# Routed experts, attention, routed experts on one core: the order of work at the start of the first expert loop, and where the first plane of results is added in the last stage

## What is computed

```
x = x + 0.5 * ffn(layernorm(x))
x = x + attention(layernorm(x))      # 16 heads of 16
x = x + 0.5 * ffn(layernorm(x))      # same weights as the first

ffn(x):                              # M = 2048 tokens, H = 256, 16 experts
  t      = x * rsqrt(mean(x*x) + eps) * norm_w
  logits = t @ gate_w.T + gate_b ;  4 best of 16, softmax over the 4 -> G
  h      = t @ w1[e].T + b1[e]       # 512 wide: a = even, b = odd columns
  act    = min(a,7) * sigmoid(1.702*min(a,7)) * (clip(b,-7,7) + 1)
  y      = act @ w2[e].T + b2[e]
  return x + sum over the 4 chosen e of G[e] * y
```

## Time and profile before

| what | us |
|---|---|
| three runs | 806.88, 807.64, 803.91 (median 806.88) |
| the profiled execution, its own time | 807.14 |
| its span in the trace | 804.4 (granted TensorE clock 0.976) |
| TensorE matmuls busy | 702.1 (87%) |
| VectorE busy | 586.4 (73%) |
| ScalarE busy | 440.1 (55%) |
| GpSimd busy | 403.1 (50%) |
| chain that ended last: TensorE / time in which the engine waited for nothing shown / GpSimd / VectorE | 30% / 8% / 8% / 8% |

### The profile page before, as it was taken

The page is one execution under the profiler, slowest core; times in us unless marked ns, Lnnn a source line. Parts: engine busy times, 40 slices in busy tenths (PEclk is TensorE's granted clock), DMA queues, the critical chain, the costliest instruction groups (busy, mean ns, idle before and its releaser), DMA issues.

```text
span 804.4 us, 18633 instructions
## 1 busy us (share of the span) xinstructions
PE 702.1 (87%) x4754; PEld 556.0 (69%) x4754; DVE 586.4 (73%) x1360; ACT 440.1 (55%) x1066; POOL 403.1 (50%) x449
## 2 busy tenths in 40 slices
PE   2576757899999999789999999988699999999995
PEld 2453436678788888666677777656478888888872
DVE  3868365977677777647778988867777777777777
ACT  3664434655555555426777676755245555555551
POOL 6667763445545555463235532447425555555552
PEclk9999879999999999999999999999899999999998
DMA  7949897768986553264444334147656877886776
GB/s 299 388 191 365 300 374 263 241 189 289 330 271 217 205 188 117 85 247 167 157 158 165 142 143 152 58 171 248 219 174 219 272 260 261 272 279 201 230 255 242
DMA packets 77919, 181.06 MB, mean 225 GB/s; under 512 B 12016, under 2 KB 36864, under 8 KB 73856
## 3 DMA queue, kind: packets, MB, share of 16 engines
q1 hardware_dynamic: 38176, 94.44, 34.3%
q0 software_dynamic: 14928, 49.97, 16.6%
q10 hardware_dynamic: 24720, 35.47, 13.6%
HBM read 97.60 MB, written 65.45 MB: 203 GB/s over the span
## 4 chain that ended last, share of the span: by engine, by line
PE 30%; issue 8%; POOL 8%; DVE 8%; DMA 1%; ACT 1%; ACTq 0%; DVEq 0%; POOLq 0%
PE s_psT L1149 7%; POOL kbuf L1361 5%; PE s_psG L1173 3%; PE s_psS L1700 3%; PE s_psO L1735 3%; DVE s_a_nm L1968 3%; PE s_psG L1672 2%; POOL rows L1593 2%; POOL s_e_own_bc L1373 1%; PE s_psT L1716 1%; PE s_psG L1685 1%; PE s_psS L1116 1%; PE s_psT L1720 1%; PE s_psS L1130 1%; DMA rows<-s_a_row,s_a_slot_i 1%
## 5 line engine op out<-in xcount | busy, mean ns | idle before, releaser
L1361 POOL DMA_INDIRECT kbuf<-f_e_ys,f_e_place x79 | 80.4, 1018 | 100.9 <-ACT f_e_ys L1308 84.6
L1149 PE MATMUL f_bank<-weights,f_e_th 128*128 x316 | 120.3, 479 | 6.7 <-issue 3.5
L1361 POOL DMA_INDIRECT kbuf<-s_e_own_ys,s_e_own_place x79 | 79.2, 1003 | 92.0 <-ACT s_e_own_ys L1308 79.4
L1149 PE MATMUL s_psT<-s_e_own_weights,s_e_own_th 128*128 x316 | 114.4, 464 | 2.9 <-ACT s_e_own_th L1333 2.1
L1593 POOL DMA_INDIRECT rows<-s_a_row,s_a_slot_i x64 | 63.8, 996 | 75.8 <-DVE s_a_slot_i L2095 58.9
L1968 DVE TENSOR_REDUCE s_a_nm<-s_psS 128x4 f32<-128x1024 f32 x64 | 78.2, 1222 | 26.3 <-PE s_psS L1700 25.7
L1214 DVE TENSOR_TENSOR s_e_own_hb<-s_psT,s_e_own_bias 128x512 f32<-128x512 f32 x79 | 54.3, 687 | 48.3 <-PE s_psT L1149 48.2
L1214 DVE TENSOR_TENSOR f_e_hb<-f_bank,f_e_bias 128x512 f32<-128x512 f32 x79 | 54.2, 686 | 43.4 <-PE f_bank L1149 43.2
L714 POOL DMA_INDIRECT rows<-f_r_row,f_r_slot_i x64 | 66.1, 1033 | 34.1 <-issue 17.9
L1149 PEld LDWEIGHTS f_bank<-weights,f_e_th 128*128 128x128 f32 x316 | 62.3, 198 | 29.9 <-issue 11.8
L2234 ACT ACTIVATE s_a_pT<-s_psT 128x1024 f32<-128x1024 f32 x62 | 63.4, 1022 | 30.5 <-PE s_psT L1720 30.0
(11 more groups left out here) (396 smaller groups left out, 1801.8 us busy)
## 6 DMA issues: line engine op xcount, KB each, us to landing
s_e_own_weights<-w_split SPq DMA_DIRECT2D x12, 1024.0 KB, 5.4
s_e_tb<-rows ACTq DMA_DIRECT2D x80, 144.0 KB, 3.2
w_split<-weights ACTq DMA_DIRECT2D x7, 1536.0 KB, 6.2
f_e_tb<-rows ACTq DMA_DIRECT2D x66, 144.0 KB, 2.5
s_a_qs<-s_a_qk SPq DMA_DIRECT2D x32, 256.0 KB, 2.5
weights<-w_raw SPq DMA_DIRECT2D x10, 768.0 KB, 13.7
w_split<-weights POOLq DMA_DIRECT2D x5, 1536.0 KB, 7.7
s_a_ks<-s_a_qk SPq DMA_DIRECT2D x30, 256.0 KB, 2.9
```

The lines of the kernel that those rows point to most:

```text
L1149: last = pe.matmul(psH[j][:, :], left[:, p % 2, j, k * P:(k + 1) * P], weights[:, h:len_units + h - SLOT + 1, k * I2:(k + 1) * I2][:, bass ...
L1361: pool.indirect_dma_start(out=kbuf[:, :], out_offset=bass.IndirectOffsetOnAxis(ap=place[:, i % KEPT:i % KEPT + 1], axis=0), in_=ys[:, n, : ...
```

## The change

It has two parts.

**The first loop and its routing.**
- Four of the scatters of ranks 2 and 3 are sent earlier: rank 2 and rank 3 of tile 0 after the first group, rank 2 of tiles 1 and 2 after the third.
- GpSimd no longer waits for rank 3 and the padding and passes nothing on for it; SyncE waits for rank 3's own semaphore where a pair needs it (a register computed from the need), and for the padding before its first fetch. GpSimd waits for all rows before its load of expert 13, now at step 5 (was 4).
- EARLY is 9: SyncE fetches pairs 0 to 8, ScalarE from pair 9 on. SyncE fetches pairs 2 to 8 before it turns to expert 4's weights; the raw weights of expert 11 are loaded after pair 4, those of 12 after pair 6.
- Expert 8 is split ahead of the loop (ScalarE before its last gates, VectorE after expert 3), and the splits of 9 and 10 and the stores of 8, 9, 10 come one step earlier.
- The table has two lines instead of one packed line in the first ffn: first spot and second spot, each with the expert in the high bits, and TensorE loads eight registers of each in every fourth step. The ready semaphores count in steps of 64, so that the loaded number is itself the value to wait for. The second ffn uses the expert's number with `% 4` and `% 5` on a ring of 15 units; `th` and `tl` lie in the two units of it that hold no weights. Register loads of more than eight are cut in two on SyncE.

**The drain of the second loop.** VectorE adds plane 0 to the six token groups inside the loop, three in step 40 and three in step 41, each time behind al. After the loop it starts with plane 1.

```diff
-NEED, EARLY = 3 * NT + 2 * NE + TOP * RINGS, 7
+NEED, EARLY = 3 * NT + 2 * NE + TOP * RINGS, 9
+SPOT2 = NEED + 2 * EARLY
...
     def landed(self, engine, stage):
...
-        if stage == TOP - 2:
-            engine.wait_ge(self.s_pad[1], 16 * (NE - FIRST))
         engine.sem_inc(self.s_landed, 1)
...
+    SENT_BETWEEN = (((0, 2), (0, 3)), (), ((1, 2), (2, 2)), (), ())
...
+            for n, k in SENT_BETWEEN[g]:
+                send(n, k)
         for k in (2, 3):
-            for n in range(TT):
+            left = [n for n in range(TT) if not any((n, k) in some for some in SENT_BETWEEN)]
+            for n in left:
                 send(n, k)
-                if n == 1:
+                if n == left[1]:
                     routed.landed(pool, k - 2)
-        routed.landed(pool, 2)
...
         split.low(dve, 3)
+        split.low(dve, 8)
...
         pad_rows(act, m.phase, table, rows, c, s_pad, FIRST, some=range(NE // 2, NE))
+        split.high(act, 8)
...
-        split.weights = own.sb("weights", [P, RING_UNITS, UNIT], fp32r)[:, :, :]
+        with ExitStack() as freed:
+            split.weights = freed.enter_context(own.nc.sbuf_tensor(f"{own.phase}_weights", [P, SECOND_RING, UNIT], fp32r))[:, :, :]
+        own.sb("ring", [P, SECOND_RING - SLOT, UNIT], fp32r)
...
-    HIGH_AT = {(-1, 0): ((8, 0),), (-1, 1): ((8, 1), (8, 2)), (0, 0): ((9, 0),), (0, 1): ((9, 1), (9, 2)),
-               (1, 0): ((10, 0),), (1, 1): ((10, 1), (10, 2)), (2, 0): ((11, 0),), (2, 1): ((11, 1), (11, 2)),
+    HIGH_AT = {(-1, 0): ((9, 0),), (-1, 1): ((9, 1), (9, 2)), (0, 0): ((10, 0),), (0, 1): ((10, 1), (10, 2)),
+               (2, 0): ((11, 0),), (2, 1): ((11, 1), (11, 2)), (4, 0): ((12, 0),), (4, 1): ((12, 1), (12, 2)),
...
         for j in range(2):
-            queue.wait_ge(routed.s_landed, need[j])
+            if first_layer:
+                third = queue.snap(need[j] & (need[j] >> 1)).with_bounds(min_val=0, max_val=1)
+                queue.wait_ge(routed.s_landed, (need[j] >> 1) + 1)
+                carry(queue, s_carry)
+                queue.wait_ge(routed.s_scat[TOP - 2], third * (16 * (T // P - 1)) + 16)
+            else:
+                queue.wait_ge(routed.s_landed, need[j])
...
+            routed.other_rows(sp)
             for p in range(2):
                 early_fetch(sp, at, p, landed[2 * p:2 * p + 2], s_carrys)
             ready_direct(NBUF - 1)
             split.load(sp, 10)
...
+            for p in range(2, BY_SP):
+                early_fetch(sp, at, p, landed[2 * p:2 * p + 2], s_carrys)
+                if p in SP_LOADS:
+                    split.load(sp, SP_LOADS[p])
...
-                at = pe.snap((spot >> 5) & 31).with_bounds(min_val=0, max_val=len_units - SLOT)
-                pe.wait_ge(s_ready1, (spot & 31) + 1)
+                if first_layer:
+                    at = pe.snap(spot & ((1 << SPOT_BITS) - 1)).with_bounds(min_val=0, max_val=UNITS - SLOT)
+                    pe.wait_ge(s_ready1, spot)
+                else:
+                    at = pe.snap(spot % NBUF)
+                    pe.wait_ge(s_ready1, spot + 1)
...
                 expert.load(s // (BANK // 2))
+                if first_layer:
+                    second_spot.load(s // (BANK // 2))
...
                 dve.tensor_tensor(al[:, b, :, :], psA, ah[:, b, :, :].bitcast(fp32), ALU.subtract).then_inc(s_al, 1)
+                if not first_layer and s in (NP, NP + 1):
+                    split.early_sums(dve, s - NP)
...
+    def early_sums(dve, half):
+        if half == 0:
+            early.append(Chain(dve, s_vd))
+            dve.wait_ge(s_in[0], 16 * NG)
+        for g in range(half * MINE // 2, (half + 1) * MINE // 2):
+            early[0].done(dve.tensor_tensor(xs[g], xs[g], planes[0][g], ALU.add))
...
-        for k in range(TOP - 2):
+        for k in range(1, TOP - 2):
```

More of the change, by code:

```diff
@@ L46, with packed @@
 SECOND_UNITS = (2, 5, 8, 11, 12)
+SPOT_BITS, TURN, SECOND_RING = 6, 100, 5 * SLOT
 HOMES = {11: SLOT, 12: 2 * SLOT, 13: KEPT_AT, 14: KEPT_AT + SLOT, 15: 0}
 def spots(first_layer):
[L52 to L58, removed]
+    if not first_layer:
+        return [(SLOT * (e % 4), SLOT * (e % 5) + 2) for e in range(NE)]
+    return [(HOMES[e], HOMES[e] + 2) if e in HOMES else (RING_AT + SLOT * (e % 4), RING_AT + SECOND_UNITS[e % 5]) for e in range(NE)]
+def packed(part):
+    return [(e << SPOT_BITS) + spot[part] for e, spot in enumerate(spots(True))]
 class Count:
@@ L1036, in _ @@
             needs = [sp.alloc_register(f"{m.phase}_sp_need{p}") for p in range(2 * BY_SP)]
[L1037 to L1038 removed]
+            bounded = lambda some: [sp.snap(r, min_val=1, max_val=TOP - 1) for r in some]
+            sp.load(needs[0:4], table[0:1, NEED:NEED + 4])
+            landed = bounded(needs[0:4])
             at = Column(sp, "so", 0, NE * REGION)
+            routed.other_rows(sp)
             for p in range(2):
@@ L1043, in _ @@
             split.load(sp, 10)
+            for first in range(4, 2 * BY_SP, 8):
+                last = min(first + 8, 2 * BY_SP)
+                sp.load(needs[first:last], table[0:1, NEED + first:NEED + last])
+                landed += bounded(needs[first:last])
+            for p in range(2, BY_SP):
+                early_fetch(sp, at, p, landed[2 * p:2 * p + 2], s_carrys)
+                if p in SP_LOADS:
+                    split.load(sp, SP_LOADS[p])
+            at.free()
+            for register in needs:
+                sp.free_register(register)
         begins = [sp.alloc_register(f"{m.phase}_begin{e}") for e in range(NBUF, NE + 1)]
-        sp.load(begins, table[0:1, 2 * NT + NE + 1:2 * NT + NE + 1 + NE - NBUF + 1])
+        for first in range(0, len(begins), 8):
+            some = begins[first:first + 8]
+            sp.load(some, table[0:1, 2 * NT + NE + 1 + first:2 * NT + NE + 1 + first + len(some)])
         tiles_before = [sp.snap(r, min_val=1, max_val=NT) for r in begins]
@@ L1074, in _ @@
         next_second(NBUF)
-        if BY_SP:
-            for p in range(2, BY_SP):
-                early_fetch(sp, at, p, landed[2 * p:2 * p + 2], s_carrys)
-            at.free()
-            for register in needs:
-                sp.free_register(register)
-            split.load(sp, 11)
-            split.load(sp, 12)
         for e in range(NBUF, NE):
```

129 lines of the change are left out of this document (84 added, 45 removed), and 4 rows, old and new, of tables (HIGH_AT, LOW_AT).

## The result

The changed kernel took 811.45 us (median of 15 runs, 808.78 to 815.11), the kernel before on the same chip 807.64 (15 runs). The ratio is 1.0049, interval 1.0032 to 1.0066: half a per cent slower, where 797.5 had been forecast. The profiled execution has a span of 809.7 us against 804.4, 5.3 more.

A forecast was written before the change was run, and what follows sets the result against it. TensorE's own queue was taken to bound both loops deep in, and late rows, weights and scatters the stretch from 80 to 130 us. -11.0 + 4.0 - 2.4 = -9.4 from 807.14 gave 797.7, set to 797.5; range 789 to 804.5.

The forecast's parts named there:

- the price of TensorE's second register load: First loop, every fourth step: 0.5 us a block in eight blocks, +4.0 us, bounds 0 to 15.7.
- The rival on the slower side: TensorE's second register load costs 1.96 us in each of ten blocks, 19.6 in all: 813.3 us; chance 0.06.
- the prediction's upper bound: First loop: the second register load costs at most 1.96 us a block, from the longest load before.
- About one load of 0.7 us fits and a second does not: TensorE's queue, first loop: one register load per block is hidden behind matmuls, a second is not.
- The queue orders at the head: SyncE fetches pairs 7 and 8 at 124.1; pair 6's bias addition comes at 130.2 instead of 141.20: -11.0 us.
- The scatters: Head, GpSimd: four sends move into waiting gaps; rank 2 lands 3.9 us earlier, rank 3 5.2 us earlier, at 124.1.
- the second rival: Head: rows land 3.9 us after the last send instead of 7.1, giving 794.5 us; chance 0.12.
- The first fetch: Head: SyncE's first fetch, now waiting for the padding, comes at 81, 1.5 us late.
- the slack of 6 us: Head: pairs 0 to 5 done by 124.5, scatters last by 6 us, covering the costs at the head.
- the landing of pair 2's rows: Head: pair 2's rows leave about 5.5 us earlier; with delays against that, pair 1's bias addition comes at 97, not 99.01.
- The drain: End of second loop: last al 1.32 us late, six sums of 3.72 us gone behind it: -2.4 us, bounds -3.7 to +1.3.
- the 0.6 us worked out from that rule: Drain: by the skill's SBUF rule the last clip waits behind three sums, making the sum 0.6 us higher; not adopted.

The follow-up runs named there:

- the four beside it: The changed kernel with one packed line, or its second line at column 336, each without and with the padding wait moved: 793.32, 796.88, 793.15, 793.65 us.
- two here: The kernel before with a second, unused register load on TensorE, from column 80 or 82: 808.23 and 807.27 us; the trace shows ten loads, not twenty.
- at column 322: The changed kernel with one packed line, TensorE alone reading a copy of that line at column 322 in the first loop: 811.58 us, ratio 1.0028.
- the run with the load moved: The changed kernel with TensorE's load of the second line two steps later, its column unchanged: 807.74 us, ratio 1.0003.

## Why the prediction was wrong

**The step that failed is the price of TensorE's second register load**, put at 0.5 us in each of eight blocks, +4.0. From pair 7 on the changed kernel takes 186.02 us, and the same kernel with its line at column 336 takes 170.34: 15.7 us, 1.96 a block. The rival on the slower side (813.3) had named this load as the place of the loss and missed the time by 2 us; it was given 0.06. The argument for the low end was that the median row, 707 ns, was nearest. A median over loads of a line at one address was carried to a line at another. All ten loads of before lay well; the row could not show what a badly placed one costs. That the lines lie differently, at columns 80 and 322, stands in the code, and the sum left it out.

That the measured 1.96 us a block equals the prediction's upper bound is luck. The bound came from the longest of the ten well-placed loads, the one at 217.7 us in the sixth block. Every trace with well-placed loads has one of 1.8 to 2.2 us in that block (the second row is the kernel with its second line at column 336):

```profile
L988 PEldq TENSOR_LOAD <-all_table x1: 1960/1960/1960, 217.7 to 217.7; - x1
...
L1015 PEldq TENSOR_LOAD <-all_table x1: 1818/1818/1818, 207.2 to 207.2; - x1
```

It says nothing of the address. Nor is the loss even: pair by pair against the kernel with its second line at column 336, the block with the stop of 4.49 us loses 5.8 us, that of pair 8 loses 2.7 and the other six 1.3 to 1.8 each. And the rival's 813.3 was added up from ten blocks (its own sum has eight, which gives 809.4) and from 11.0 us gained at the head, where 7.9 were.

Nor was the price right for what it described. With the second line well placed, the second load costs 170.34 - 170.23 = 0.1 us over eight blocks by the traces, 0.9 us by the ratios (0.9857 and 0.9846, whose intervals overlap), not to be told from nothing: it is hidden. "About one load of 0.7 us fits and a second does not" was wrong. Two of 0.6 fit, and one of 2.1 does not.

**The queue orders at the head: right in kind, 3 us short.** -7.9 at pair 7, -8.0 at pair 6, where -11.0 was taken. SyncE issues seven pairs ahead of expert 4's second weights, ScalarE no longer stands on the raw weights of 11 (though they leave at 99.73, not near 93), as forecast. The scatters gave less than their count: GpSimd passes the wait for ranks 0 and 1 at 80.07 instead of 79.38 and goes on with rank 3 at 100.82 instead of 103.34, 2.5 us earlier, not 3.9, and its last send ends 3.5 us earlier, not 5.2. Against that the rows of rank 3 landed within 3.1 us of it instead of 7.12: what the second rival said (3.9) did come true. It gained nothing, as pair 6 no longer waited for them.

The first fetch was put at 81, by 3 us of landing for the padding, and came at 83.57: ScalarE's padding issues ended at 79.47 instead of 78.20, and 4.1 us passed behind them. And the slack of 6 us between the pairs and the scatters wasn't there. Five pairs behind pair 1 stands pair 6, which the pairs alone were to bring at 124.5; they bring it at 133.19. Pair 1 is at 103.28, not 97, as its wait for pair 2's rows ends at 100.68, and five pairs take 29.9 us, not 27.5. The step that failed here is the landing of pair 2's rows, taken as no longer than before (3.3 us) and measured at 9.6 to 12.8 us in the changed kernel and the four beside it. The 49.2 us that the prediction has between first fetch and pair 6 (81 to 130.2) agree with the traces (48.0 to 50.5) by luck: it had put the scatters there. With the padding wait moved and the line aligned, the fetch is at 80.30 and pair 6 at 130.11.

**The drain: right in kind, at least 1 us too much.** al of the last pair is at 793.14; taken back by the 6.73 us by which the loop is late, that is 786.41, 1.62 after the earlier trace rows instead of 1.32. The whole drain gained 1.4, not 2.4, and 0.35 where the sums were put alone into the kernel before. The bound that bites is one the prediction passed over with "were done before VectorE's": TensorE's two groups come behind the last pair's products. Taken against the loop, ScalarE copies them out 2.0 us later than before (the last at 804.29 - 6.73 = 797.56 instead of 795.58), and their copies and store now end level with VectorE's, so the six sums taken from behind can't all count. The clip beside the sums is the only one of forty that is longer:

```profile
L1446 POOL TENSOR_SCALAR s_e_own_bc<-s_e_own_hb x40: 608/612/755, 591.6 to 787.4; 128x512 f32<-128x512 f32 x40
```

0.755 us instead of 0.61, and the three sums beside it take 2.30 us against 1.93 for the three that have no clip beside them. It is so in each of the kernels with early sums (752 to 757 ns). The prediction read the earlier trace rows wrongly: in the kernel before not one of these 40 clips stands beside a VectorE instruction with two SBUF operands, so the row could say nothing of a conflict. The first loop of the same trace could have. Here are, from the changed kernel, VectorE's last operation of a low part and a clip of the first loop, then the clip and the second sum of the drain:

```profile
165.16 0.68 DVE L484 TENSOR_TENSOR weights<-weights 128x512 fp32r<-128x512 f32 x1
165.24 1.08 POOL L1446 TENSOR_SCALAR f_e_bc<-f_e_hb 128x512 f32<-128x512 f32 x1
...
787.41 0.76 POOL L1446 TENSOR_SCALAR s_e_own_bc<-s_e_own_hb 128x512 f32<-128x512 f32 x1
787.61 1.10 DVE L2494 TENSOR_TENSOR all_x<-all_x,s_own_late 128x512 f32<-128x512 f32 x1
```

A clip that begins beside such an instruction ends 0.47 to 0.48 us after it, whether its own record is 0.61 us long or 1.08; and the VectorE instruction that begins beside the clip takes 1.10 us instead of 0.68 and ends 0.54 to 0.55 us after the clip. That holds in each such pair of all the traces here, those of the kernel before included. The records overlap, but each holds the wait for the other: they take turns. The Trainium skill, SBUF — State Buffer, Who interferes with whom, has two such instructions contend for an exclusive lock, and the trace agrees. Only the price was less than the 0.6 us worked out from that rule, as the clip came between the first and the second sum and not behind the third: al of the last pair is 1.62 us late instead of 1.32.

**What held**: the second loop neither gained nor lost (458.10 against 458.06 us from the last addition of the first to its own). That the two agree so closely is chance, as this stretch is 456.3 to 461.7 us in the other traces, the slower round aside. The forecast, which knew nothing of the load's address, is 797.5, and the changed kernel with that address mended takes 796.88. That agreement is luck: the head gave 3 us less, the load cost 4 less, and the drain gave 1 less.

## What to carry to other kernels

Before a new line is put into a table that an engine loads registers from, work out the byte at which it begins and keep every load at a multiple of 16; here 8 bytes cost 15 us, as much as all the other edits together had gained. Take the price of a new operation from a row only if operand addresses and placement are alike as well as its kind, and if a rival names the mechanism with a measured maximum of its own, ask what would make each instance that maximum before giving it a small chance. Before a row is read as "no conflict", look whether the two instructions ever ran side by side in it, and remember that a long record can hold a wait. And count an experiment's instructions in its trace before reading its time: two here had lost the very loads that they were to price.

## What was not expected of the hardware

A load of eight registers takes 0.59 us at its fastest from a 16-byte multiple and 1.94 from 8 bytes past one. At the same place it also takes much longer at times: 4.285 us in the changed kernel, 4.726 at column 322, 8.079 in the run with the load moved. Well-placed loads are long at times too: 1.8 to 2.2 us in the sixth block of every trace that has them, and 1.8 to 3.0 in the second block of the four traces that have the head of the kernel before. What a load then waits for isn't shown; in the stretch of the first of them, the 4.285 us, the DMA engines are busy at 0.90.

Such a stop costs more than its length. In the changed kernel TensorE stands for 4.49 us at 214 us, and its granted clock is at half, the 1.2 GHz level, for what follows, before it is at full (2.4 GHz) again:

```profile
214.00:218.00 4.00, 0.09 (x1) 0.00 (x0) 0.97 (x2) 0.99 (x2) 2.57 (x3) 0.98 0.90 344
218.00:222.00 4.00, 3.42 (x10) 2.60 (x11) 0.00 (x0) 0.46 (x1) 0.00 (x0) 0.50 0.73 219
...
226.00:230.00 4.00, 4.00 (x26) 3.31 (x25) 2.04 (x4) 2.34 (x9) 2.58 (x3) 1.00 0.37 107
```

A first product takes 0.79 us there instead of 0.49, and this pair is 11.51 us behind the one before it instead of 5.1. The stops of 1.0 to 2.8 us at the other blocks from 120 us on are followed by matmuls of 0.49 to 0.50 us, at the full clock.
